# A selective scan's first state with reciprocals in y's blocks and its product on GpSimd, and the skip term made among the experts

## The reference, cut to what matters

```
def _selective_scan(u, delta, A, Bm, Cm, D):
    deltaA = einsum('bld,dn->bldn', delta, A)
    deltaBu = einsum('bld,bld,bln->bldn', delta, u, Bm)
    cum = exp(flip(cumsum(flip(shifted(deltaA)))))
    x = deltaBu * cum
    x = cumsum(x, axis=1) / (cum + 1e-12)
    out = einsum('bldn,bln->bld', x, Cm)
    return out + u * D
...
h = x_after_attention                       # window attention, its projection
h = h + selective_scan(layernorm(h), ...)
h = h + experts(layernorm(h), ...)          # one of 32 small experts for each token
```

## Time and profile before

| | |
|---|---|
| median of 3 runs (us) | 604.15 (603.57 to 606.45) |
| the profiled execution (us) | 605.85, its span 604.1 |
| PE busy, share of the span | 90% |
| DVE | 81% |
| ACT | 67% |
| POOL | 58% |
| mean granted clock of PE | 0.96 |

### The profile page before, as it was taken

The page is one execution under the profiler, slowest core; times in us unless marked ns, Lnnn a source line. Parts: engine busy times, 40 slices in busy tenths (PEclk is TensorE's granted clock), DMA queues, the critical chain, the costliest instruction groups (busy, mean ns, idle before and its releaser), DMA issues. The chain is left out here.

```text
span 604.1 us, 18372 instructions
## 1 busy us (share of the span) xinstructions
PE 542.7 (90%) x7273; PEld 389.6 (65%) x7274; DVE 491.1 (81%) x910; ACT 403.3 (67%) x723; POOL 350.0 (58%) x388
## 2 busy tenths in 40 slices
PE   5897999999999999999657757579999999999996
PEld 4897889998989989997212223345555555555553
DVE  3888788888888888886799999768888878788873
ACT  3676788888888888888697576124545455454543
POOL 8306377777777777774898598553333343333320
PEclk9899999999999999999788798869999999999999
DMA  9732222222222222210000000000101101010111
GB/s 193 113 51 47 63 60 55 62 58 63 61 55 61 60 57 63 58 35 3 1 0 0 0 1 1 3 2 18 26 22 23 24 20 26 20 26 20 26 23 27
DMA packets 62382, 23.06 MB, mean 38 GB/s; under 512 B 45780, under 2 KB 62292, under 8 KB 62292
## 3 DMA queue, kind: packets, MB, share of 16 engines
q1 hardware_dynamic: 61200, 21.63, 17.6%
q10 hardware_dynamic: 964, 0.20, 0.2%
q0 software_dynamic: 128, 0.00, 0.0%
HBM read 5.02 MB, written 4.19 MB: 15 GB/s over the span
## 5 line engine op out<-in xcount | busy, mean ns | idle before, releaser
L772 DVE TENSOR_REDUCE work<-psum 128x16 f32<-128x1024 f32 x64 | 78.1, 1220 | 29.4 <-PE psum L604 29.4
L707 ACT ACTIVATE work<-work 128x1024 f32<-128x1024 f32 x64 | 67.8, 1060 | 21.6 <-DVE work L777 21.6
L777 DVE TENSOR_TENSOR work<-psum,work 128x1024 f32<-128x1024 f32 x64 | 78.4, 1225 | 2.2
L715 ACT ACTIVATE work<-psum 128x512 f32<-128x512 f32 x128 | 70.9, 620 | 2.4 <-PE psum L619 1.5
L619 PE MATMUL psum<-kc,work 128*128 128x128 f32 x512 | 67.6, 275 | 4.3 <-ACT work L707 3.5
L1687 POOL TENSOR_TENSOR m_rstd<-m_var,m_mhalf 128x4 f32<-128x4 f32 x32 | 32.2, 1008 | 61.8 <-DVE m_var L1897 61.8
L1798 ACT ACTIVATE hid<-psum,b1c 128x512 f32<-128x512 f32 x96 | 58.9, 684 | 13.2 <-PE psum L1702 13.2
L635 PEld LDWEIGHTS psum<-work 128*64 128x64 f32 x2048 | 62.3, 138 | 5.3 <-issue 5.3
L635 PE MATMUL psum<-work 128*64 128x18 f32 x2048 | 65.5, 212 | 0.0
L619 PEld LDWEIGHTS psum<-kc,work 128*128 128x128 f32 x512 | 58.8, 141 | 8.8 <-ACT work L707 4.5
L1710 PE MATMUL psum<-x_t,w1x 64*64 64x256 f32 x1024 | 64.4, 391 | 0.0
(11 more groups left out here) (198 smaller groups left out, 1285.2 us busy)
## 6 DMA issues: line engine op xcount, KB each, us to landing
work<-big_bc SPq DMA_DIRECT2D x256, 32.0 KB, 2.0
h_all<-in_x SPq DMA_DIRECT2D x16, 256.0 KB, 5.3
work<-big_a SPq DMA_DIRECT2D x32, 128.0 KB, 2.2
out<-out_st SPq DMA_DIRECT2D x126, 32.0 KB
w1x<-in_L_ffn_W SPq DMA_DIRECT2D x2, 128.0 KB, 3.6
kc<-constants SPq DMA_DIRECT2D x1, 202.0 KB, 2.9
w2x<-in_L_ffn_W SPq DMA_DIRECT2D x1, 128.0 KB, 3.3
work<-in_L_tok_qkv_w ACTq DMA_DIRECT2D x2, 32.0 KB, 3.3
```

The source lines that it names most:

```text
L707: act.activation(prob[:, f], prob[:, f], ACT.Exp).then_inc(prob_done, 1)
L715: act.activation(prob_t[:, f, 4 * half:4 * half + 4, :].rearrange("p j q -> p (j q)"), banks[4 + half][:, :], ACT.Copy).then_inc(prob_t_do ...
L772: dve.tensor_reduce(top[:, f, :].rearrange("p (g h) -> p g h", g=4), sc, AX.X, ALU.max).then_inc(top_done, 1)
L777: dve.tensor_tensor(prob[:, f].rearrange("p (g h) k -> p g h k", g=4), sc, top[:, f, :].rearrange("p (g h) -> p g h", g=4).unsqueeze(3).br ...
```

## The change

For the first state, the reciprocals of block q are written to y's block q in SBUF. POOL multiplies them there by the scanned block (`times_rec`), and DVE multiplies that by C in place (`times_c`), one block behind its sums. PE spreads B two blocks ahead, into banks 0, 1 and 5, 6 in turn. ACT's `skipped` and POOL's `add` of the first state are gone; the second state still has its `add`. The skip term u*D + bias is made by ACT for each quad among the experts (`stage_skip`, into the new buffer `skip_st`), and `stage_y`, now on POOL, adds it to y into `y_st`. In PE's turn, y is turned ahead of `xh`, and the marks of ACT's half and y go to other places in PSUM. ACT's copy of `o_t` comes right behind its three activations of `hid`.

```diff
+    def log_of(q):
+        return even_buf if isinstance(q, int) and q < BLOCKS and q % 2 else odd_buf
+
+    def rec_of(q):
+        return block_of(y, q) if isinstance(q, int) and q < BLOCKS else rec_bank
+
+    def b_of(q):
+        return psum[:, 5:7, 0:BLK] if isinstance(q, int) and q < BLOCKS and q % 2 else psum[:, 0:2, 0:BLK]
...
+            if k == 1:
+                pe.wait_ge(tail_gain, 4)
+            if k > 1:
+                pe.wait_ge(term_done, k - 1)
+            for half in range(HALVES):
+                m = pe.matmul(b_of(k)[:, half, :], w_b[0][:, :],
+                              u[:, half * L + k * BLK:half * L + k * BLK + BLK], start=True, stop=True)
+            m.then_inc(b_done, 1)
...
+        def spread_c(k):
+            if k > 0:
+                pe.wait_ge(out_done, k)
+            for half in range(HALVES):
+                m = pe.matmul(psum[:, 2 + half, 0:BLK], w_c[0][:, :],
+                              u[:, half * L + k * BLK:half * L + k * BLK + BLK], start=True, stop=True)
+            m.then_inc(c_done, 1)
...
         with pe.If(alive_of[0][0] > 0):
+            spread_b(0)
+            spread_b(1)
             for k in range(BLOCKS):
-                body(k, k, w_b[0], w_c[0])
+                spread_c(k)
+                if k < BLOCKS - 2:
+                    spread_b(k + 2)
...
         def recip(q):
             act.wait_ge(lnc_done, q + 1)
-            if isinstance(q, int) and q == 0:
+            if isinstance(q, int) and q < BLOCKS:
+                act.wait_ge(delta_done, CH)
+            else:
                 act.wait_ge(tail_gain, 4)
-            else:
                 act.wait_ge(ratio_done, q)
-            act.activation(psum[:, 5:7, 0:BLK], log_cum, ACT.Exp, scale=-1.0).then_inc(rec_done, 1)
-
-        def whole(q, scale, after):
+                act.wait_ge(term_done, q)
+            act.activation(rec_of(q), log_of(q), ACT.Exp, scale=-1.0).then_inc(rec_done, 1)
...
+        def times_rec(blk):
+
+            pool.wait_ge(sum_done, blk + 1)
+            pool.wait_ge(rec_done, blk + 1)
+            pool.tensor_tensor(block_of(y, blk), block_of(y, blk), cums[blk % RING], ALU.mult).then_inc(ratio_done, 1)
...
         with pool.If(alive_of[0][0] > 0):
             duc(0, 0, 0)
+            duc(1, 1, 1)
+            tail_product(0)
             for k in range(BLOCKS - 1):
-                duc(k + 1, k + 1, (k + 1) % RING)
-                add(k, k)
-                if 1 <= k < 5:
+                times_rec(k)
+                if k < BLOCKS - 2:
+                    duc(k + 2, k + 2, (k + 2) % RING)
+                if 2 <= k < 5:
                     tail_product(k - 1)
...
-        def body(q, r, fresh):
+        def add_up(q, r, fresh):
...
+            dve.tensor_tensor(a, a, b_of(q), ALU.mult).then_inc(term_done, 1)
             dve.wait_ge(term_done, q + 1)
             for half in range(HALVES):
                 first = 0.0 if fresh else cums[(r - 1) % RING][:, half, BLK - 1:BLK]
                 m = dve.tensor_tensor_scan(a[:, half, :], unit.to_broadcast([P, BLK]), a[:, half, :],
                                            first, ALU.mult, ALU.add)
             m.then_inc(sum_done, 1)
+
+        def times_c(blk):
+
+            dve.wait_ge(ratio_done, blk + 1)
+            dve.wait_ge(c_done, blk + 1)
+            dve.tensor_tensor(block_of(y, blk), block_of(y, blk), psum[:, 2:4, 0:BLK], ALU.mult).then_inc(out_done, 1)
...
         with dve.If(alive_of[0][0] > 0):
-            whole(0)
-            carry(0, (BLOCKS - 1) % RING)
+            add_up(0, 0, True)
+            for k in range(1, BLOCKS):
+                add_up(k, k % RING, False)
+                times_c(k - 1)
+            carry(0, (BLOCKS - 1) % RING, BLOCKS)
         with dve.Else():
...
-                body(BLOCKS, BLOCKS % RING, True)
-                carry(1, BLOCKS % RING)
+                add_up(BLOCKS, BLOCKS % RING, True)
+                carry(1, BLOCKS % RING, BLOCKS + 1)
+                kept_back()
+                finish(BLOCKS, BLOCKS % RING)
...
@@ -1673,9 +1753,20 @@
         @block.gpsimd
         def _(pool):
             pool.memset(mhalf[:, :], -0.5).then_inc(power_set, 1)
-            pool.tensor_copy(ident_b[:, :], ident).then_inc(masks_set, 1)
+
+            def stage_y(i):
+
+                pool.wait_ge(skip_made, i + 1)
+                if not first(i):
+                    pool.wait_ge(y_turned, i)
+                pool.tensor_tensor(y_st[:, :, :].rearrange("p k (r x) -> p k r x", r=8),
+                                   skip_st[:, :, :].rearrange("p k (r x) -> p k r x", r=8),
+                                   raster(y, i // 2 * 512 + i % 2 * 32), ALU.add).then_inc(y_staged, 1)
+
+            stage_y(0)
             pool.tensor_scalar(off[:, :, :], kc[:, K_EYE:K_EYE + NE].unsqueeze(2).to_broadcast([P, NE, HID]),
                                1.0, BIG, ALU.subtract, ALU.mult).then_inc(masks_set, 1)
...
@@ -1683,6 +1774,9 @@
                     return
                 pool.wait_ge(xc_done, i + 1)
                 pool.tensor_tensor(sq[:, :, :], xc[:, :, :], xc[:, :, :], ALU.mult).then_inc(sq_done, 1)
+                if i == 0:
+                    pool.tensor_copy(ident_b[:, :], ident).then_inc(masks_set, 1)
+                    stage_y(2)
...
+                    stage_y(i + 3)
 
             steps(pool, body)
 
...
                     pe.wait_ge(chosen, i - 1)
-                    pe.wait_ge(h_done, min(i + 1, QUADS))
+                    pe.wait_ge(lg_done, i - 1)
...
-                            m = pe.matmul(psum[0:96, (2, 6)[b], 256 * b + k * P:256 * b + k * P + P],
+                            m = pe.matmul(psum[0:96, (1, 6)[b], 256 + k * P:256 + k * P + P],
...
                     m.then_inc(o_turned, 1)
-                if live(i, 1):
-
-                    pe.wait_ge(xh_done, i)
-                    if not first(i, 1):
-                        pe.wait_ge(lg_done, i - 1)
-                    for n in range(2):
-                        m = pe.transpose(psum[:, 1, n * P:n * P + P], xh[:, 2 * n:2 * n + 2, :], ident)
-                    m.then_inc(x_turned, 1)
                 if live(i, -1):
                     pe.wait_ge(y_staged, i + 2)
                     if not first(i, -1):
                         pe.wait_ge(h_done, i + 1)
+                    for n in range(2):
+                        m = pe.transpose(psum[:, 2, n * P:n * P + P], y_st[:, n, :], ident)
+                    m.then_inc(y_turned, 1)
+                if live(i, 1):
+
+                    pe.wait_ge(xh_done, i)
                     if live(i, 2):
                         pe.wait_ge(mark_act, i - 1)
                     for n in range(2):
-                        m = pe.transpose(psum[:, 2, 256 + n * P:256 + n * P + P], y_st[:, n, :], ident)
-                    m.then_inc(y_turned, 1)
+                        m = pe.transpose(psum[:, 1, n * P:n * P + P], xh[:, 2 * n:2 * n + 2, :], ident)
+                    m.then_inc(x_turned, 1)
                 if live(i, 2):
                     if first(i, 2):
                         pe.wait_ge(masks_set, 2)
...
-            def stage_y(i):
-                act.activation(y_st[:, :, :].rearrange("p k (r x) -> p k r x", r=8),
-                               raster(y, i // 2 * 512 + i % 2 * 32), ACT.Copy).then_inc(y_staged, 1)
+            def stage_skip(i):
+                act.activation(skip_st[:, :, :].rearrange("p k (r x) -> p k r x", r=8),
+                               raster(u, i // 2 * 512 + i % 2 * 32), ACT.Identity, bias=bias_col[:, 0:1],
+                               scale=d_col[:, 0:1]).then_inc(skip_made, 1)
 
             def body(i):
                 if live(i, 2):
                     act.wait_ge(mark_turned, i * 2 - 3)
-                    act.activation(mark_t[:, 0, :], psum[0:96, 2, 0:256], ACT.Copy).then_inc(mark_act, 1)
+                    act.activation(mark_t[:, 0, :], psum[0:96, 1, 256:512], ACT.Copy).then_inc(mark_act, 1)
...
                     relu(i, 3)
-                if live(i, -2):
-                    if i >= -1:
-                        act.wait_ge(y_turned, i + 2)
-                    stage_y(i + 2)
                 if live(i, 2):
                     act.wait_ge(o_done, i * 2 - 2)
                     if not first(i, 2):
                         act.wait_ge(o_turned, i - 2)
                     act.activation(o_t[:, :, :].rearrange("p k t -> p (k t)"), psum[:, 6, 0:256], ACT.Copy
                                    ).then_inc(o_copied, 1)
-
+                if live(i, -3):
+                    act.wait_ge(y_staged, i + 3)
+                    stage_skip(i + 3)
+
```

More of the change, by code:

```diff
@@ L1176, in last_block @@
             recip(q)
-        def nothing(k):
-            pass
-        def skipped(k):
-            act.activation(block_of(y, k), block_of(u, k), ACT.Identity, bias=bias_col[:, 0:1], scale=d_col[:, 0:1]).then_inc(y_set, 1)
         mine = (cum_done, lnc_done, rec_done)
@@ L1187, in _ @@
```

(16 more changed lines are left out.)

73 lines of the change are left out of this document (53 added, 20 removed).

## The result

The changed kernel takes **713.48 us** (median of 4 runs, 712.5 to 714.29), the kernel before 605.09 (4 runs, 603.57 to 606.45): a ratio of 1.1784, 95% interval 1.1761 to 1.1807. The forecast was 697 in a range of 657 to 713. The sign and the mechanism came as written; the time lies half a microsecond above the range.

A forecast was written before the change was run, and what follows sets the result against it. PE alone was taken to bound the experts, DVE the scan with POOL almost as full. Ring 57.4, clock 33.6, start 1.5 and scan 0 gave 92.5 on the profiled 605.85, 698.4; by the median 697 us, range 657 to 713.

The forecast's parts named there:

- the ring: Experts: masks wait on y's turning, POOL's `stage_y` and square, then DVE's sum; 2.05 us a turn, 28 turns, 57.4 us.
- the clock: Experts: PE's pause of 2.1 us a turn lowers its granted clock; 1.2 us a turn, 33.6 us, bounds 0 and 48.
- the experts' start: Before the first marks: `stage_y(0)` and `stage_y(1)` behind `off` delay the first turning and square; +1.5 us, bounds 0.7 and 3.
- the scan: Scan: block 7's term 7.4 us earlier with POOL as bound, lost again in the tail; 0 us, bounds -2.4 and +2.5.
- no circle: Rival, experts: y turned in time for POOL's body, so nothing waits; 603 us, chance 0.03.
- three falls in four turns: Experts: assumed rate of clock falls behind PE's pause, 0.75 x 1.6 = 1.2 us a turn over 28 turns.
- a fall costs about 1.6 us: Price of one fall of PE's clock, from scan matmuls taking 3.66 and 3.47 us instead of 1.96.
- a fall in every turn: Rival, experts: a clock fall in every turn, or two, 28 x 1.7 to 2.0 us; 711 to 720 us, chance 0.12.
- the thin work ahead of the pause: Experts: only four marks and six turnings, 1.2 us, precede PE's pause; reason for assuming more falls than four of six.
- six pauses behind full work: Scan of the kernel before: PE pauses of 2.00 to 2.48 us; the clock fell behind four and stayed up behind two.
- mostly under DVE's two sums: Experts' start: the identity's cast and `stage_y(2)` precede `rstd`, mostly hidden by DVE's two sums; within the +1.5 us.
- one and a half falls for three spreads: Scan's tail: one and a half clock falls of 1.6 us on three PE spreads give back the 2.4 us gain.

The follow-up runs named there:

- experiment 1: Changed kernel, but POOL takes y two quads ahead instead of three, so its wait was already met a turn ago: 609.67 us, ratio 1.0074 to the kernel before.
- Experiment 3: Changed kernel plus four unused PE matmuls of 256 columns between the turning of xh and the masks: 678.6 us, ratio 1.1211 to the kernel before.
- experiment 4: Changed kernel plus two unused PE matmuls, not four, between the turning of xh and the masks: 692.83 us, ratio 1.1441 to the kernel before.
- experiment 6: On experiment 1, the constants `off` and `ident_b` made by DVE instead of POOL: 609.85 us, ratio 1.0064 to the kernel before.
- Experiment 7: On experiment 1, PE spreads B of state 1 ahead of C of block 7: 603.83 us, ratio 0.9975 to the kernel before.
- 8: Changed kernel with y two quads ahead, constants on DVE, and B of state 1 ahead of C of block 7: 603.98 us, ratio 0.9973.
- experiment 10: On experiment 9, POOL takes y of quads 2 and 3 right behind the squares of quads 0 and 1: 600.67 us, ratio 0.9928.
- experiment 2: Changed kernel, y still three quads ahead, but POOL's square of the next quad stands ahead of the wait for y: 609.46 us, ratio 1.0083.
- experiment 9: On 8, PE's sum over the tail's states moved into its pause ahead of C of state 1: 600.23 us, ratio 0.9926 to the kernel before.

## Where the prediction held, and which step failed

The time came out 16.5 us above the forecast, 0.9 of it because the kernel before has a median of 605.09 now and 604.15 then. The experts' turns can be taken apart by the first and last marks, the groups of one line (count, duration in ns, first and last start). Before:

```profile
L1734 PE MATMUL psum<-ident_b,mark x128: 218/220/258, 402.8 to 594.8; 128*96 128x128 bf16 x128
```

after:

```profile
L1830 PE MATMUL psum<-ident_b,mark x128: 219/219/257, 407.6 to 703.2; 128*96 128x128 bf16 x128
```

and with the pause filled:

```profile
L1830 PE MATMUL psum<-ident_b,mark x128: 219/219/257, 407.2 to 668.2; 128*96 128x128 bf16 x128
```

That is 192.0, 295.6 and 261.0 us; without the unused matmuls of the last three turns, the last is 255.8. Another 1.4 us of it are the first turn, where the unused matmuls held the masks back (4.60 - 3.19). So the ring costs 255.8 - 1.4 - 192.0 = 62.4 us and the clock 295.6 - 254.4 = 41.2, of which 2.2 are the first turn's.

| term | predicted | measured |
|---|---|---|
| the ring, 28 turns | 57.4 | 62.4 |
| the clock | 33.6 | 41.2 |
| the experts' start | 1.5 | 2.4 |
| the scan | 0 | 1.9 |
| sum | 92.5 | 107.9 (the medians: 108.4) |

Each measured value lies inside the bounds that the prediction gave it, and all four lie above the value taken. The clock's is the largest miss (7.6 us), then the ring's (5.0).

- **The circle.** Right in each member, in the count of 28 turns and in the end, where the last turns are free. The rival "no circle" is what experiment 1 makes of the kernel. The size was low, 3.44 us from marks to masks instead of 3.26, and 8.41 instead of 8.25 for the turn: POOL started 0.53 behind the turning of y instead of 0.42, and the square started 0.68 behind the start of `y_st` instead of 0.61, as `y_st` took 0.73. I had taken the square's time for an operation of the same size and engine; no row showed one of POOL in the pattern of the image, in which `y_st` is read and written, and no run shows what the 0.12 us more come from. The rest of the 5.0 us is one turn of 8.72 and last turns that are 0.2 longer than before.
- **The clock: the step that failed.** "I take three falls in four turns" and "a fall costs about 1.6 us": the price was right (10.04 - 8.41 = 1.63; in the kernel before, PEclk is 0.50 from 338 to 341, inside the spread of 3.66 us), the number was not. The clock fell in 25 of 28 held turns, 41.2 us instead of 33.6, and my range had no room for that beside the other terms that were low. The rival "a fall in every turn", with 711 to 720 us and a chance of 0.12, is the one that the result bears out. I had a point for it in hand, the thin work ahead of the pause (1.2 us of marks and turnings), which no run tested; I used it as an argument against six pauses behind full work, and then still took the rate nearly from those six. Experiment 3 shows that the pause causes the falls behind the first turn, 24 of the 25 (the first turn's fall was there with the pause filled too), and experiment 4 how sharply they depend on it: behind the first turn it fell in none of 27 turns with 0.43 us of pause (once 0.73), in 11 with 1.29 (once 1.60), and in 24 with 2.15 or a little more.
- **The experts' start.** 14.55 instead of 12.2 us from the memset to the first marks, 2.4 against 1.5, inside the bounds. `off` ahead of `y_st(1)` was seen, and is a quarter to a third of it (0.8 us in experiment 6, 0.6 from 7 to 8); and what I had as "mostly under DVE's two sums" is POOL's `y_st` that runs ahead of the square and beside `m_xc` (0.75, experiment 10). The last part, about 1.0, is the new pair at the very start: PE's first turning of y comes 394.55 - 393.08 = 1.47 us behind the memset, behind ACT's 0.60 and POOL's 0.72, where it came 0.5 behind it with ACT's copy alone.
- **The scan.** Right in its shape: the gain of seven us at the term of block 7 (366.8 predicted, 367.24 seen) and its loss in the tail. State 1's term was 378.72 and not 375.7, since both spreads ahead of it ran with the clock fallen (3.73 and 3.11 us, at 0.50 and 0.59 granted, instead of 2.1 and 2.0). I had charged one and a half falls for three spreads, and the three of them fell. Experiment 7 shows that the tail's order was the cause: 5.8 us for one swap.

The change's idea for the scan was sound, then, and its table of turns in the experts was not: with y taken two ahead and B ahead of C it is 603.83 against 605.65 us (an interval that only just leaves out no change), and with the constants on DVE and the sum in the pause 600.23 against 604.75.

Open stays what decides in which of several equal turns the clock falls. The runs show that it does not take every pause alike (experiment 4), not why.

## What to carry to other kernels

Before an operation with a wait is moved ahead in an in-order queue, read what stands behind it: the wait here was harmless for 27 times out of 27 once the square stood in front of it (experiment 2), and cost 104 us with the square behind. Where PE gets a pause in each turn of a loop, price the clock as a fall in every turn as the upper case, unless the profile shows turns as thin that hold (here 24 of 27 fell); and try cheap work in the pause, useful if there is any (the sum of experiment 9), unused if not (experiment 3).
